# Attention slots of a gated cross-attention block: the product with the values placed ahead of the turns and projections on TensorE

## The chip, the core and the metric

The kernel runs on one core of a Trainium2 chip. The metric is device time in microseconds (us), the median of three runs. TensorE (PE in the profile) multiplies, VectorE (DVE), ScalarE (ACT) and GpSimd (POOL) work elementwise, and SyncE (SP) issues transfers. Each engine takes its own list of instructions in the order in which the program gives them, and they meet only at semaphores.

## The reference

`x` has 2 batches of 512 tokens of width 128; the context has 2 x 32 tokens of width 128. Queries come from the normalised `x`; keys and values come from the normalised context and from the normalised `x` itself. There are 16 heads of 64.

```
xn, ln = layernorm(ctx), layernorm(layernorm(x))
q = ln @ Wq
k, v = split(concat([xn @ Wkv, ln @ Wkv], axis=1))
sim  = rmsnorm(q) * scale @ rmsnorm(k).T
attn = softmax(sim)
x = x + tanh(g_xattn) * ((attn @ v) @ Wout + bout)
x = x + tanh(g_ffn) * moe(layernorm(x))      # 8 experts of width 256, top 2 of 8
```

The whole kernel works with each float32 operand split in a high and a low half of 16 bits, so one product in full precision is three matmuls (high by high, high by low, low by high).

## The kernel before, in words

**Units and slots.** A unit is 4 heads of one batch; there are 8 units of 8 slots, 64 attention slots in all (`SLOTS`). Slot n works on head `n % 8 // 2` of unit `n // 8` and on one half of its 512 keys. Each engine has a function `slot(n)`, and its list is the unrolled loop over n; the tables `qk_at`, `t_at`, `v_at`, `cs_at`, `nm_at` and `cst_at` say what else is done in which slot. So the order of the work is written out by hand.

**What TensorE does in slot n, before.** First the transposed scores of slot n: four matmuls (lines 1234, 1235) into `st_ps`, which wait until ScalarE has taken slot n-1's out of it (`exp_ok`). Then `score(j)`, two matmuls (line 1175) for the row maxima of a slot 11 later. Then, in even slots up to 44, `turn_tile`: four transposes (line 1163) of a projected and normalised tile of queries and keys, into `tv`; and in even slots up to 42 `project_tile`: three matmuls (lines 1093 to 1095) for the tile that is turned two slots later, into `pj`. In every other odd slot the three matmuls make values instead. Then `times_values(n - 2)`: 16 matmuls of the exponentials' high half (lines 1150, 1151), 8 of their low half (line 1156), and in odd slots 12 more for the context. The low half is waited for right before line 1156 (`plo_ok`). In slots 8u+4 and 8u+5 follow the context's scores and the turn of the maxima, in slots 8u the context's transposed scores.

**What follows a turn and a projection.** ScalarE in slot n takes the exponential of slot n (line 656), then the high halves of the turned tile (lines 603, 604), then the squares of the projected tile (line 589). VectorE in slot n divides a finished head (lines 963, 970), takes the maxima of `score` (line 941), the low halves of the turned tile (line 840), the sums of squares (line 819) and the mean squares (line 823). In slot n+1 GpSimd raises the mean squares to the power -1/2 (`inverse_rms`, line 439), and VectorE multiplies the projected tile by the result (`normalise_qk`, line 829), which slot n+2's turn waits for. In slots with new values VectorE takes their low half behind that (line 985).

**GpSimd's list** in slot n is: `inverse_rms` of slot n-1's projection, if there was one; then the low half of slot n-1's exponentials, `p_lo` (line 516); in slots 8u+2 also the low half of the context's exponentials, `pc_lo` (line 522). It takes the rms first and the low half second, in this order.

**After slot 44** there are no turns of queries and keys; the attention's output is turned and projected, and experts follow (lines 1358 to 1377 on TensorE, 560 on GpSimd).

Of the kernel before, what the change touches and what calls it, by code (L numbers as in the profile page):

```python
# [21 lines left out]
def flamingo_gated_block(nc, x, ctx_in, mask, g_xattn, g_ffn, ln_x_g, ln_x_b, ln_l_g, ln_l_b, qn_g, kn_g,  # L22
# [20 lines left out]
    with ExitStack() as ctx:  # L43
# [149 lines left out]
        def need(eng, s, count):  # L193
            if count > 0:
                eng.wait_ge(s, count)
# [38 lines left out]
        def need_lo(eng, k):  # L234
            on_dve, on_pool = lo_counts(k)
            need(eng, lo_ok, on_dve)
            need(eng, lop_ok, on_pool)

        def need_vlo(eng, k):
            need(eng, vlop_ok, min(k, QT))  # L240
            need(eng, vlo_ok, k - QT)

        def is_slot(n):
            return 0 <= n < SLOTS
# [13 lines left out]
        def o_part(G, q):  # L258
            return o_ps[G % 2][:, (DH + 1) * q:(DH + 1) * (q + 1)]
# [812 lines left out]
        def _(pe):  # L1072
# [13 lines left out]
            def project(out_ap, toks, w):  # L1086

                if isinstance(w, tuple):
                    hi, lo = (m[:, :].rearrange("p (g k c) -> p g k c", g=NG, k=3)[:, w[0]:w[0] + w[1], 2, :]
                              for m in (wqkv_hi, wqkv_lo))  # L1090
                else:
                    hi, lo = wqkv_hi[:, w], wqkv_lo[:, w]
                nc.tensor.matmul(out_ap, lnT_hi[:, toks], hi, start=True, stop=False)
                nc.tensor.matmul(out_ap, lnT_hi[:, toks], lo, start=False, stop=False)
                return nc.tensor.matmul(out_ap, lnT_lo[:, toks], hi, start=False, stop=True)
# [50 lines left out]
            def values(o_of, ph, cols, vh, vl, start):  # L1146

                for q in range(QT):
                    c = slice(cols.start + q * P, cols.start + (q + 1) * P)
                    nc.tensor.matmul(o_of(q), ph[:, c], vh, start=start and q == 0, stop=False, skip_group_check=True)  # L1150
                    nc.tensor.matmul(o_of(q)[:, 0:DH], ph[:, c], vl, start=False, stop=False, skip_group_check=True)  # L1151

            def values_lo(o_of, pl, cols, vh):
                for q in range(QT):
                    c = slice(cols.start + q * P, cols.start + (q + 1) * P)
                    last = nc.tensor.matmul(o_of(q), pl[:, c], vh, start=False, stop=True, skip_group_check=True)  # L1156
                return last

            def turn_tile(tau):
                pe.wait_ge(norm_ok, tau + 1)  # L1160
                tr = turn_bank(tau)
                for c in range(4):
                    last = nc.tensor.transpose(tr[:, c * P:(c + 1) * P], qk[tau % 2][:, c * P:(c + 1) * P], ident[:, :])  # L1163
                last.then_inc(qkT_ok, 1)

            def score(j):
                u, c, q = j // 8, j % 8 // QT, j % QT
                if j == 0:
                    pe.wait_ge(norm_ok, QT)
                if j % 8 == 0:  # L1170
                    pe.wait_ge(hi_ok, QT * (u + 1))
                need(pe, mx_ok, j)
                for r in range(2):
                    rows = slice(DH * r, DH * (r + 1))
                    last = nc.tensor.matmul(s2_ps[:, 512 * r:512 * (r + 1)], HL[u % 2][rows, 0, c, q * P:(q + 1) * P],  # L1175
                                            HL[u % 2][rows, 0, 2 + c, :], start=True, stop=True)
                last.then_inc(s_ok, 1)
# [9 lines left out]
            def times_values(m):  # L1187
                u, h, i = m // 8, m % 8 // 2, m % 2
                G = m // 2
                if i == 0:  # L1190

                    need(pe, o_ok, G - 1)
                    if h == 0:
                        pe.wait_ge(cexp_ok, u + 1)
                    if h == 2 and u + 1 < UNITS:
                        pe.wait_ge(nmc_ok, u + 2)
                need_vlo(pe, QT * (u // 2) + 2 * i + 2)
                pe.wait_ge(exp_ok, m + 1)

                def o_of(q):  # L1200
                    return o_part(G, q)

                for k in range(2):
                    v = V[u // 2 % 2][:, 2 * i + k, HG * (u % 2) + h, :]
                    values(o_of, p_hi[m % NP], slice(512 * k, 512 * (k + 1)), v[:, 0:DH + 1], v[:, DH + 1:VW],
                           i == 0 and k == 0)
                if i == 1:
                    v = Vbd[u % 2][:, h, :]
                    if h == 0:
                        pe.wait_ge(vbd_ok[u % 2], 64 * (u // 2 + 1))  # L1210
                        pe.wait_ge(cplo_ok, u + 1)
                    values(o_of, pc_hi[u % 2], slice(0, 512), v[:, 0:DH + 1], v[:, DH + 1:VW], False)
                    values_lo(o_of, pc_lo[u % 2], slice(0, 512), v[:, 0:DH + 1])
                pe.wait_ge(plo_ok, m + 1)
                for k in range(2):
                    v = V[u // 2 % 2][:, 2 * i + k, HG * (u % 2) + h, :]
                    last = values_lo(o_of, p_lo[m % NP], slice(512 * k, 512 * (k + 1)), v[:, 0:DH + 1])
                last.then_inc(pv_ok, 1)

            def slot(n):  # L1220
# [17 lines left out]
                j = s_pair(n)  # L1238
                if j is not None:
                    score(j)  # L1240
                if n in t_at:
                    tau = t_at[n]

                    need_lo(pe, tau)

                    need_vlo(pe, len([m for m in v_at if m < n]))
                    if n > LN1_AT + 4:
                        pe.wait_ge(lnT_ok, 3)
                    turn_tile(tau)
# [12 lines left out]
                if n in v_at:  # L1262
# [7 lines left out]
                        pe.wait_ge(wlo_ok, NG)  # L1270
                    g, first = 2 * w % NG, 2 * w // NG * N + t * P
                    project(tv[:, :], slice(first, first + P), (g, 2)).then_inc(v_mm, 1)
                if is_slot(n - 2):
                    times_values(n - 2)
                if n == CTX_AT:

                    pe.wait_ge(wlo_ok, NG)
# [103 lines left out]
            for n in range(FIRST, LAST):  # L1381
                slot(n)
                if n in (SLOTS, SLOTS + 1):
                    gate_up(n - SLOTS)
# [47 lines left out]
```

## Time and profile before

| | us |
|---|---|
| median of 3 runs | 387.31 (385.56 to 388.3) |
| the profiled execution | 387.43 |
| its span in the trace | 385.6 |
| TensorE busy | 320.4 |
| GpSimd busy | 256.5 |
| VectorE busy | 292.4 |
| turn of slot 4 to turn of slot 44 | 89.66 to 220.64 |

In the rows a time is in microseconds from the span's start. A row of the timeline gives the start, the duration, the engine, the line of the kernel, the operation, the tile written, the tiles read, their shapes and, in square brackets, how long the engine sat idle before it and what ended that. A matmul's duration is longer than the distance to the next, because they are pipelined, so distances between starts tell TensorE's pace. A matmul over 512 columns in the attention stage follows the one before by 0.22 us.

### The profile page before, as it was taken

To read this page: it belongs to the slowest core of one execution; us is meant where nothing else is said; L and a number is where in the kernel's file an instruction comes from. 1 tells how busy PE (TensorE), PEld (TensorE's weight loads), DVE (VectorE), ACT (ScalarE), POOL (GpSimd) and SP (SyncE) were. 2 spreads that over 40 slices of the span, in tenths; PEclk is the share of its full clock that TensorE was granted. 3 is DMA by queue.
4 is the path that set the end of the run, shared out by engine and by line. 5 is a ranking of instruction groups with operands and counts; after the bars stand their busy time and mean duration, and the time that the engine had idled before them with its cause. 6 is when DMAs were issued, how large, how long until landed. Compare 5 with 4: busy or idle time off the path is not lost.

```text
span 385.6 us, 9369 instructions
## 1 busy us (share of the span) xinstructions
PE 320.4 (83%) x3641; PEld 197.9 (51%) x3641; DVE 292.4 (76%) x578; ACT 195.3 (51%) x329; POOL 256.5 (67%) x197
## 2 busy tenths in 40 slices
PE   1563756789999999999999999899865999965993
PEld 0131423346556556555555656687543787533662
DVE  4874756769888898888898974646796677888895
ACT  2532434555665565656555645366824454624451
POOL 7695368478797897888887987356932334523453
PEclk9956686789999999999999999999996999999999
DMA  6316000620530611603406116730000000001000
GB/s 191 92 30 134 3 7 2 133 42 2 117 60 5 149 27 25 148 6 86 91 6 141 33 29 145 225 112 3 2 2 0 2 2 0 3 0 29 0 3 28
DMA packets 31470, 20.38 MB, mean 53 GB/s; under 512 B 11650, under 2 KB 30914, under 8 KB 31426
## 3 DMA queue, kind: packets, MB, share of 16 engines
q1 hardware_dynamic: 30482, 19.75, 22.4%
q8 instruction: 29, 0.48, 0.5%
q10 hardware_dynamic: 944, 0.04, 0.2%
q14 instruction: 15, 0.12, 0.1%
HBM read 5.87 MB, written 0.52 MB: 17 GB/s over the span
## 4 chain that ended last, share of the span: by engine, by line
POOL 31%; issue 28%; PE 22%; DVE 12%; ACT 4%; DMA 1%; POOLq 1%; DVEq 0%; ACTq 0%
POOL p_lo L516 18%; POOL p_lo L560 5%; POOL rms_r L439 3%; PE pj L1128 3%; DVE wqkv_hl L1033 2%; PE tv L1163 2%; POOL pc_lo L522 2%; PE tv L1113 1%; DVE sumsq L819 1%; PE big L1358 1%; PE big L1360 1%; POOL v L534 1%; PE big L1359 1%; PE big L1234 1%; DVE qk L829 1%
## 5 line engine op out<-in xcount | busy, mean ns | idle before, releaser
L516 POOL TENSOR_TENSOR p_lo<-p 128x1024 f16<-128x1024 f32 x64 | 121.9, 1924 | 17.2 <-ACT p L656 13.3
L656 ACT ACTIVATE p<-big 128x1024 f32<-128x1024 f32 x64 | 65.6, 1025 | 66.0 <-PE big L1235 63.9
L941 DVE TENSOR_REDUCE nm_main<-big 128x2 f32<-128x1024 f32 x64 | 78.2, 1222 | 20.2 <-PE big L1175 19.8
L560 POOL TENSOR_TENSOR p_lo<-p,p_lo 128x512 f16<-128x512 f32 x32 | 37.1, 1159 | 58.6 <-ACT p_lo L735 56.3
L439 POOL TENSOR_TENSOR rms_r<-meansq,power 128x8 f32<-128x8 f32 x32 | 52.3, 1638 | 29.1 <-DVE meansq L823 28.3
L1234 PE MATMUL big<-w 128*128 128x512 f16 x128 | 48.8, 381 | 2.7 <-ACT p L656 2.7
L1235 PE MATMUL big<-w 68*128 68x512 f16 x128 | 48.7, 380 | 0.0
L1150 PEld LDWEIGHTS o_ps<-v,p 128*128 128x128 bf16 x512 | 35.9, 99 | 9.4 <-issue 4.1
L1150 PE MATMUL o_ps<-v,p 128*128 128x65 f16 x512 | 40.7, 194 | 0.0
L1151 PE MATMUL o_ps<-v,p 128*128 128x64 f16 x512 | 40.6, 195 | 0.0
L1151 PEld LDWEIGHTS o_ps<-v,p 128*128 128x128 bf16 x512 | 34.4, 98 | 5.5 <-issue 0.3
L1175 PE MATMUL big<-hl 64*128 64x512 f16 x128 | 26.0, 402 | 9.2 <-DVE nm_main L941 9.2
L1046 DVE SCALAR_TENSOR_TENSOR p<-p,big 128x512 f32<-128x512 f32 x32 | 21.8, 683 | 15.0 <-ACT p L730 14.9
L1163 PE MATMUL tv<-ident,qk 128*128 128x128 f32 x116 | 20.8, 307 | 14.8 <-DVE qk L829 8.1
L1358 PE MATMUL big<-x2T_hi,gu_hi 128*128 128x512 f16 x64 | 25.2, 394 | 8.7 <-DVE p L1050 8.7
L1373 PE MATMUL o_ps<-wd_hi,p_lo 128*128 128x128 f16 x128 | 23.8, 223 | 8.6 <-POOL p_lo L560 5.6
L730 ACT ACTIVATE p<-big 128x512 f32<-128x512 f32 x32 | 18.9, 594 | 22.0 <-PE big L1360 20.7
L819 DVE TENSOR_REDUCE sumsq<-squares 128x8 f32<-128x512 f32 x32 | 21.7, 678 | 9.0 <-ACT squares L589 8.9
L1156 PE MATMUL o_ps<-v,p_lo 128*128 128x65 f16 x512 | 26.2, 194 | 0.3 <-POOL p_lo L516 0.3
L1163 PEld LDWEIGHTS tv<-ident,qk 128*128 128x128 f32 x116 | 13.5, 152 | 22.9 <-issue 20.0
L1359 PE MATMUL big<-x2T_lo,gu_hi 128*128 128x512 f16 x64 | 25.3, 395 | 0.0
L1360 PE MATMUL big<-x2T_hi,wqkv_hl 128*128 128x512 f16 x64 | 25.1, 391 | 0.0
(206 smaller groups left out, 758.7 us busy)
## 6 DMA issues: line engine op xcount, KB each, us to landing
w<-hl SPq DMA_DIRECT2D x64, 128.0 KB, 3.4
w<-hl SPq DMA_DIRECT2D x16, 256.0 KB, 3.9
hl<-n_kernel_gating_EDF_dram SPq DMA_DIRECT2D x1, 1024.0 KB, 5.8
hl<-L_ffn_kernel_up_EDF_dram SPq DMA_DIRECT2D x1, 1024.0 KB, 5.4
o_sb<-in_L_xattn_Wkv_dram SPq DMA_DIRECT2D x2, 384.0 KB, 7.2
x_sb<-in_x_dram SPq DMA_DIRECT2D x2, 256.0 KB, 4.0
wout<-in_L_xattn_Wout_dram SPq DMA_DIRECT2D x1, 512.0 KB, 4.8
k1c<-kc_hl SPq DMA_DIRECT2D x32, 8.0 KB, 1.8
```

The source lines that it names most:

```text
L439: nc.gpsimd.tensor_tensor(rms_r[:, tau % QT, :], meansq[:, tau % QT, :], power[:, 0:8], ALU.pow).then_inc(rr_ok, 1)
L516: nc.gpsimd.tensor_tensor(p_lo[m % NP][:, :], p[m % NP][:, :], p_hi[m % NP], ALU.subtract).then_inc(plo_ok, 1)
L560: nc.gpsimd.tensor_tensor(hid_lo[m % NH], hid[m % NH], hid_hi[m % NH], ALU.subtract).then_inc(hlo_ok, 1)
L656: nc.scalar.activation(p[n % NP][:, :], st_ps, ACT.Exp).then_inc(exp_ok, 1)
L941: nc.vector.tensor_reduce(nm_main[:, u % 2, 2 * c:2 * c + 2, q], s2_ps.rearrange("p (k n) -> p k n", k=2), AX_X, ALU.max, negate=True).the ...
L1150: nc.tensor.matmul(o_of(q), ph[:, c], vh, start=start and q == 0, stop=False, skip_group_check=True)
L1151: nc.tensor.matmul(o_of(q)[:, 0:DH], ph[:, c], vl, start=False, stop=False, skip_group_check=True)
L1163: last = nc.tensor.transpose(tr[:, c * P:(c + 1) * P], qk[tau % 2][:, c * P:(c + 1) * P], ident[:, :])
L1234: nc.tensor.matmul(o, w1[:, 2 + h // 2, h % 2, keys], w1[:, h // 2, h % 2, :], start=True, stop=False)
L1235: last = nc.tensor.matmul(o, w2[0:M_ROWS, 2 + h // 2, h % 2, keys], w2[0:M_ROWS, h // 2, h % 2, :], start=False, stop=True)
L1358: nc.tensor.matmul(o, gu_hi[k][:, w], x2T_hi[:, toks], start=True, stop=False)
L1359: nc.tensor.matmul(o, gu_hi[k][:, w], x2T_lo[:, toks], start=False, stop=False)
```

## The change

`times_values(n - 2)` stands right behind `score(j)`, ahead of the turn and of the projections. Nothing is added or removed, and the other engines' lists stay as they are. In slots without a turn or a projection the order is the same as before.

```diff
@@ -1238,6 +1238,8 @@
                 j = s_pair(n)
                 if j is not None:
                     score(j)
+                if is_slot(n - 2):
+                    times_values(n - 2)
                 if n in t_at:
                     tau = t_at[n]
 
@@ -1270,8 +1272,6 @@
                         pe.wait_ge(wlo_ok, NG)
                     g, first = 2 * w % NG, 2 * w // NG * N + t * P
                     project(tv[:, :], slice(first, first + P), (g, 2)).then_inc(v_mm, 1)
-                if is_slot(n - 2):
-                    times_values(n - 2)
                 if n == CTX_AT:
 
                     pe.wait_ge(wlo_ok, NG)
```

TensorE's list in slot 4 before, with the semaphores that each row waits for. Where lines are left out, the pair of lines 1150 and 1151 repeats seven times:

```order
L1175 MATMUL big<-hl 128x512
L1163 MATMUL tv<-ident,qk 128x128 [waits vlo_ok,lnT_ok,vlop_ok,norm_ok,lop_ok,lo_ok]
L1163 MATMUL tv<-ident,qk 128x128 x3
L1093 MATMUL pj<-wqkv_hl,lnT_hi 128x512 [waits norm_ok,wlo_ok]
L1094 MATMUL pj<-wqkv_hl,lnT_hi 128x512
L1095 MATMUL pj<-wqkv_hl,lnT_lo 128x512
L1150 MATMUL o_ps<-v,p 128x65 [waits exp_ok,vlop_ok]
L1151 MATMUL o_ps<-v,p 128x64
...
L1156 MATMUL o_ps<-v,p_lo 128x65 [waits plo_ok]
L1156 MATMUL o_ps<-v,p_lo 128x65 x7
L1304 MATMUL o_ps<-mask_row,ones_row 128x512 [waits o_ok,w1_ok1,kc_ok1]
```

The turn waited for the normalised tile (`norm_ok`) and for `tv` to be free (`vlo_ok`, `lo_ok`); the low half's wait (`plo_ok`) stood behind turn and projection. The same slot in the change:

```order
L1175 MATMUL big<-hl 128x512
L1150 MATMUL o_ps<-v,p 128x65 [waits exp_ok,vlop_ok]
L1151 MATMUL o_ps<-v,p 128x64
...
L1156 MATMUL o_ps<-v,p_lo 128x65 [waits plo_ok]
L1156 MATMUL o_ps<-v,p_lo 128x65 x7
L1163 MATMUL tv<-ident,qk 128x128 [waits vlo_ok,lnT_ok,vlop_ok,norm_ok,lop_ok,lo_ok]
L1163 MATMUL tv<-ident,qk 128x128 x3
L1093 MATMUL pj<-wqkv_hl,lnT_hi 128x512 [waits norm_ok,wlo_ok]
L1094 MATMUL pj<-wqkv_hl,lnT_hi 128x512
L1095 MATMUL pj<-wqkv_hl,lnT_lo 128x512
L1304 MATMUL o_ps<-mask_row,ones_row 128x512 [waits o_ok,w1_ok1,kc_ok1]
```

Now the turn and the projection stand behind the wait for `plo_ok`. GpSimd's list in slots 1 to 6, which the change leaves alone:

```order
L439 TENSOR_TENSOR rms_r<-meansq,power 128x8 [waits norm_ok,ms_ok]
L516 TENSOR_TENSOR p_lo<-p 128x1024 [waits exp_ok] x2
L522 TENSOR_TENSOR pc_lo<-pc 128x512 [waits cexp_ok]
L439 TENSOR_TENSOR rms_r<-meansq,power 128x8 [waits norm_ok,ms_ok]
L516 TENSOR_TENSOR p_lo<-p 128x1024 [waits exp_ok] x2
L439 TENSOR_TENSOR rms_r<-meansq,power 128x8 [waits norm_ok,ms_ok]
L516 TENSOR_TENSOR p_lo<-p 128x1024 [waits pv_ok,exp_ok] x2
```

In each pair of slots the rms of the even slot's projection (which waits for the mean squares, `ms_ok`) stands ahead of the low half of the even slot's exponentials.

## Rows read from the trace of the kernel before

**Rows 1.** The page, busy time of each engine over the whole span.
```profile
PE 320.4 (83%) x3641; PEld 197.9 (51%) x3641; DVE 292.4 (76%) x578; ACT 195.3 (51%) x329; POOL 256.5 (67%) x197
```

**Rows 2.** One unit: length; busy PE, PEld, DVE, ACT, POOL; clock, DMA share, GB/s.
```profile
163.80:190.00 26.20, 25.50 (x352) 15.23 (x351) 22.69 (x41) 15.31 (x24) 22.32 (x13) 1.00 0.32 66
```

**Rows 3.** Waits of 111.4 to 190 us (three units): total, times, longest.
```profile
POOL rms_r L439 <- DVE meansq L823: 11.1, 9, 1.5
...
PE tv L1163 <- DVE v L985: 1.3, 3, 0.5
...
PE tv L1163 <- issue: 0.6, 3, 0.2
```

**Rows 4.** Chain of waits of 163 to 193 us, its shares by line.
```profile
by line: POOL p_lo L516 52.2%; issue 47.5%; POOL pc_lo L522 6.6%; POOL rms_r L439 2.3%; POOLq L195 0.5%
```

**Rows 5.** Timeline of TensorE in slot 34, a slot without a wait.
```profile
187.43 0.39 PE L1175 MATMUL big<-hl 64*128 64x512 f16 x2
187.75 0.66 PE L1163 MATMUL tv<-ident,qk 128*128 128x128 f32 x4
...
188.68 0.38 PE L1095 MATMUL pj<-wqkv_hl,lnT_lo 128*128 128x512 f16 x1
...
189.39 0.40 PE L1156 MATMUL o_ps<-v,p_lo 128*128 128x65 f16 x8
...
189.63 0.38 PE L1234 MATMUL big<-w 128*128 128x512 f16 x1
```

**Rows 6.** Timeline of all engines from slot 36's score to slot 38's turn.
```profile
193.66 0.39 PE L1175 MATMUL big<-hl 64*128 64x512 f16 x2
...
194.47 0.63 PE L1163 MATMUL tv<-ident,qk 128*128 128x128 f32 x4 [0.42 <-DVE v L985]
...
195.78 0.60 ACT L589 ACTIVATE squares<-pj 128x512 f32<-128x512 f32 x1
...
197.35 0.17 DVE L823 TENSOR_SCALAR meansq<-sumsq 128x8 f32<-128x8 f32 x1
...
197.60 1.64 POOL L439 TENSOR_TENSOR rms_r<-meansq,power 128x8 f32<-128x8 f32 x1 [1.10 <-DVE meansq L823]
...
199.20 1.89 POOL L516 TENSOR_TENSOR p_lo<-p 128x1024 f16<-128x1024 f32 x1
...
201.27 0.66 PE L1163 MATMUL tv<-ident,qk 128*128 128x128 f32 x4
```

**Rows 7.** Timeline of GpSimd and VectorE in slot 35, ahead of slot 36's turn.
```profile
191.15 1.64 POOL L439 TENSOR_TENSOR rms_r<-meansq,power 128x8 f32<-128x8 f32 x1
...
192.82 0.69 DVE L829 TENSOR_TENSOR qk<-pj,rms_r 128x512 f32<-128x512 f32 x1 [0.56 <-POOL rms_r L439]
193.43 0.68 DVE L985 SCALAR_TENSOR_TENSOR v<-tv,v 128x512 f16<-128x512 f32 x1
```

**Rows 8.** Timeline of slots 1 to 3; last, the stretch's busy times and clock.
```profile
80.95 3.75 POOL L516 TENSOR_TENSOR p_lo<-p 128x1024 f16<-128x1024 f32 x2
...
81.86 1.00 PE L1163 MATMUL tv<-ident,qk 128*128 128x128 f32 x4 [0.51 <-DVE qk L829]
...
85.81 1.64 POOL L439 TENSOR_TENSOR rms_r<-meansq,power 128x8 f32<-128x8 f32 x1
...
82.00:84.00 2.00, 2.00 (x8) 1.11 (x8) 1.18 (x2) 0.83 (x3) 2.00 (x2) 0.50 0.11 21
```

**Rows 9.** Timeline of TensorE: slot 4's turn, slot 44's turn, slot 45's first matmul.
```profile
89.66 0.66 PE L1163 MATMUL tv<-ident,qk 128*128 128x128 f32 x4
...
220.64 0.63 PE L1163 MATMUL tv<-ident,qk 128*128 128x128 f32 x4 [0.40 <-DVE v L985]
...
222.67 0.38 PE L1234 MATMUL big<-w 128*128 128x512 f16 x1
```

**Rows 10.** Timeline among the experts: GpSimd's low half, then TensorE, which waited.
```profile
348.37 1.16 POOL L560 TENSOR_TENSOR p_lo<-p,p_lo 128x512 f16<-128x512 f32 x1 [5.92 <-ACT p_lo L735]
...
349.58 0.10 PEld L1373 LDWEIGHTS o_ps<-wd_hi,p_lo 128*128 128x128 f16 x1 [2.67 <-POOL p_lo L560]
```

## The prediction, made before the result was known

> **What bounds the kernel now.** I read the page first: TensorE is busy for 320.4 us of 385.6, more than any other engine [rows 1]. The change touches only slots 2 to 47, so the next view is the table of busy times by unit of 8 slots. In one unit of 26.20 us TensorE is busy for 25.50, GpSimd for 22.32 and VectorE for 22.69, at full granted clock (1.00, which is 2.4 GHz) [rows 2]. The reader is to see that TensorE sets the pace there and that GpSimd is close behind. The chain of waits for the same stretch nevertheless names GpSimd's low halves (52.2%) and "issue" [rows 4]: it follows GpSimd's own list back and does not go over to what GpSimd waited for. So I take from it only that GpSimd is nearly as tight. The table of waits says what it waited for: nine times in three units, 11.1 us in all, for VectorE's mean squares before the rms [rows 3]. TensorE's own waits ahead of a turn are small: 1.3 us in three times for VectorE's `v`, 0.6 us in three times put down to issue [rows 3], so (1.3 + 0.6) / 3 = 0.63 us a unit.
>
> The pace that I compare with: slot 4's turn starts at 89.66 and slot 44's at 220.64 [rows 9], 20 pairs of slots in 130.98 us, 6.55 us a pair.
>
> **What the change removes.** A turn that waits for VectorE would now have the values' matmuls ahead of it as cover. In slot 36 the score starts at 193.66 and the turn at 194.47 [rows 6]; in slot 34, without a wait, they are 0.32 apart [rows 5]. The values' high half and low half take, from the last projection matmul's start to the next slot, 189.63 - 188.68 - 0.22 = 0.73 us [rows 5], more than the 0.49 of delay. If nothing else came in, 0.63 us a unit would be saved, five times, and the 0.51 at slot 2 [rows 8]: 3.7 us.
>
> **What the change adds.** The low half's wait now stands ahead of the turn and the projection, in every even slot. That ties together two chains that were apart, because GpSimd takes the rms of slot n's projection ahead of slot n's low half. The new ring, from a turn to the turn two slots later, with the trace's distances:
> - Turn to rms: slot 36's turn starts at 194.47. The projection follows it, ScalarE's squares start at 195.78, the mean squares at 197.35 and the rms at 197.60, where GpSimd had sat idle for 1.10 us [rows 6]. That is 3.13 us. TensorE's part of it (turn, then projection) moves as one block, so the distance stays.
> - Rms to low half: the low half of slot 36 starts at 199.20, 1.60 us later, and takes 1.89 us [rows 6]. The exponential that it needs belongs to the slot before and is long there; the order of GpSimd's list keeps it back.
> - GpSimd to TensorE: at the only kind of place where TensorE clearly waits for GpSimd, the low half ends at 348.37 + 1.16 = 349.53 and the weight load starts at 349.58 [rows 10]. 0.05 us, and about 0.03 more to the matmul.
> - The low half's eight matmuls: 189.39 to 189.63, 0.24 us [rows 5]. Then comes slot 38's turn.
>
> The sum is 3.13 + 1.60 + 1.89 + 0.08 + 0.24 = 6.94 us. What the change of kind from the values' matmuls to the transposes costs is not shown; between score and turn the distance of 0.32 is 0.10 more than the 0.22 of 512 columns [rows 5], so it lies between 0 and 0.10. I take **6.95 us a pair**, near the lower end because the low half's hand-over may hide it.
>
> Is that ring the longest? TensorE's own work in the heaviest pair, slot 36's turn to slot 38's with the context's scores between, is 201.27 - 194.47 = 6.80 us without a wait inside [rows 6]; the mean pair has (26.20 - 0.63) / 4 = 6.39. Both are under 6.95. The old ring through VectorE's normalised tile is shorter too: from the rms at 191.15 to `v` at 193.43 and the turn at 194.47 is 3.32 [rows 6, 7], and 3.13 + 3.32 = 6.45. GpSimd's longest pair holds one rms (1.60), two low halves (2 x 1.85) and `pc_lo` (1.0): 6.3. So the new ring decides in all 20 pairs, and TensorE waits ahead of the low half: on average 6.95 - 6.39 = 0.56 us a pair. Today no ring runs through rms and low half together, since the low half is used behind the projection, and what waits behind it is not the next rms.
>
> **The terms.**
> 1. Slots 4 to 44: 20 x (6.95 - 6.55) = +8.0 us.
> 2. Start: slot 0's low half ends about 80.95 + 1.90 = 82.85 [rows 8]. Slot 2's turn was at 81.86 and can now start only behind it and the eight matmuls, which at the clock of 0.50 (1.2 GHz) in that place [rows 8] take up to twice 0.24. So the turn is 1.3 to 1.5 us later. Its rms was at 85.81, 3.95 behind the turn [rows 8], since turn and projection ran at the lower clock. If the clock is back earlier relative to the work, some of it returns. Between +0.5 and +1.5; I take +1.2, near the delay that must arise.
> 3. End: behind slot 44's turn the values (0.73) no longer stand before slot 45's first matmul, 222.67 - 220.64 = 2.03 us later today [rows 9]: -0.7 us.
> 4. Moved odd slots (the projection of values behind the product): nothing. Slot 35's `v` on VectorE stands behind the rms's `qk` anyway [rows 7], and its 3.32 us from rms to turn can grow to 3.82 before it reaches the new ring. If that cover went, each us counts once in every second pair.
>
> Sum: 8.0 + 1.2 - 0.7 = +8.5 us. The profiled execution took 387.43 us (span 385.6 and 1.8 around it), 0.1 above the median of 387.31, so the forecast is 395.9 on it and **395.8 us** on the median. Bounds: a pair of 6.80, where TensorE's heaviest pair alone decides, with a start of +0.5 gives +4.8 (392.1); a pair of 7.15, the ring with another 0.2 for each hand-over that the trace of before shows only among the experts, and a start of +1.5 give +12.8 (400.1).
>
> **The rivals.**
> - *The gain arrives* (9%): the low half is ready in time, the turns' waits vanish: 387.3 - 3.7 = 383.6 us, faster. It holds if, from a turn to the next low half, the ring is under 6.39 us. For it: the score of slot 36 at 193.66 plus 0.32 plus 0.5 of high half is 194.48, and the low half that it needs ends at about 191.15 + 1.60 + 1.90 = 194.65 [rows 6, 7], only 0.2 too late. Against it: the turn then starts later, and so do the rms and the next low half; the lateness is handed on until the pair is as long as the ring. The Trainium skill (Perfetto Trace Analysis, Identifying Performance Opportunities) says to improve the most occupied engine and to close the gaps in its row; by that, with TensorE at 25.50 of 26.20, this change would bring its 383.6. The trace speaks against it with GpSimd's share and its 11.1 us of waits.
> - *Delay is taken up* (6%): the ring lengthens by less than 0.15 a pair, or slots after 44 wait today for something that does not move. 387 to 391 us, within 1%. Against it: TensorE had no wait of length from slot 45's start on that would shrink, as far as the timeline of 222 to 236 us goes.
> - *The clock falls too* (4%): TensorE would now idle in every pair for 0.56 us of 6.95, 8%. At 0.50 slot 2's turn took 1.00 us where it takes 0.66 at full clock [rows 5, 8], and a pair's 6.39 us of work would near 10. Five of 20 pairs at that level are 5 x 3 = 15 us more: 411. Against it: clock 1.00 in the unit shown with 0.70 us of idleness in it. The Trainium skill (TensorE: Matmul & The Clock Gate, A second HAM failure mode) tells of a kernel whose clock swung because of many tiny pauses between groups of matmuls. By that rule this rival would be likely; no run here shows it yet.
> - *The ring decides*, as in the sum: 81%.
>
> **How the numbers follow.** The median is 395.8. The range 390 to 400.5 takes in both bounds and the lower edge of the second rival; outside lie the gain, most of the second rival and the clock, under 2 in 10. A measurement of this kernel tells 1% (3.9 us) from no change: its three runs lie within 0.7%. Slower by over 1% are the main case and the clock, 0.85; within 1% 0.06; faster 0.09.
>
> **What would show it.** In the new trace slots 4 to 44 should take about 139 us from turn to turn, evenly, also where no context work stands. TensorE should wait ahead of line 1156 for GpSimd's `p_lo`, in even slots only, and no more ahead of line 1163. GpSimd's wait before the rms for the mean squares should grow from 11.1 / 9 = 1.2 us to 6.95 - 1.60 - 2 x 1.87 = 1.6 us (less where `pc_lo` stands before it), its low half should start 1.60 behind the rms. The distance of turn to rms should stay 3.13. The forecast is wrong if the pairs keep 6.55, if the wait at line 1156 is absent, or if most of the difference lies after slot 45.

## The result and the profile after

| | before | after |
|---|---|---|
| median, us | 387.5 (385.56 to 388.3, 4 runs) | 396.11 (395.06 to 396.41, 4 runs) |
| the profiled execution, us | 387.43 | 395.98 |
| its span, us | 385.6 | 394.2 |
| ratio after / before | | 1.0225, 95% interval 1.0182 to 1.0267 |

The kernel before has one run more here than in the section on the time before, so its median is 387.5 and not 387.31. The forecast was 395.8, the measured median is 396.11, 2.25% slower and clear of noise. The three terms can be read off one by one. First TensorE's timeline of the change: slot 4's turn, slot 44's turn, slot 45's first matmul, which answer to [rows 9].

```profile
89.60 0.63 PE L1163 MATMUL tv<-ident,qk 128*128 128x128 f32 x4
...
229.93 0.63 PE L1163 MATMUL tv<-ident,qk 128*128 128x128 f32 x4
...
231.22 0.38 PE L1234 MATMUL big<-w 128*128 128x512 f16 x1
```

From slot 4 to slot 44 it now takes 140.33 us, 7.02 a pair, where it took 130.98 and 6.55. Slot 4's turn is as early as before, slot 45 starts 8.55 us later than before, and the span ends 8.6 later: behind slot 45 nothing was lost or regained.

One turn of the ring, slots 28 to 30, in the timeline of all engines. It answers to [rows 6].

```profile
173.77 0.63 PE L1163 MATMUL tv<-ident,qk 128*128 128x128 f32 x4
...
176.90 1.64 POOL L439 TENSOR_TENSOR rms_r<-meansq,power 128x8 f32<-128x8 f32 x1 [1.67 <-DVE meansq L823]
...
178.50 1.89 POOL L516 TENSOR_TENSOR p_lo<-p 128x1024 f16<-128x1024 f32 x1
...
180.45 0.42 PE L1156 MATMUL o_ps<-v,p_lo 128*128 128x65 f16 x8
...
180.79 0.63 PE L1163 MATMUL tv<-ident,qk 128*128 128x128 f32 x4
```

Turn to rms 3.13, rms to low half 1.60, low half to TensorE's first use of it 1.95 (1.89 and 0.06 of hand-over), that to the next turn 0.34: 7.02. ScalarE had finished the exponential that this low half needs at 173.03, 5.5 us before the low half started; GpSimd sat idle for 1.67 us ahead of the rms, with the low half behind it in its list. The table of waits, for three units of the change (117.7 to 201.8 us), shows both ends; it answers to [rows 3].

```profile
POOL rms_r L439 <- DVE meansq L823: 17.1, 12, 1.7
...
PE o_ps L1156 <- POOL p_lo L516: 5.0, 9, 0.6
```

TensorE waits for the low half 9 times in 12 pairs, 0.55 us each, and nowhere ahead of line 1163. In the other three pairs, those with the context's scores (as in the rows above), TensorE has more work of its own and arrives just as the low half does. The 12 waits of GpSimd for the mean squares are 1.67 us in nine pairs and 0.67 in the three in which `pc_lo` (1.0 us) stands ahead of the rms. The clock did not fall in this stage: here is the row of the busy times for the three units, as in [rows 2].

```profile
117.70:201.80 84.10, 78.47 (x1043) 46.12 (x1054) 66.67 (x121) 46.61 (x72) 67.05 (x40) 1.00 0.30 62
```

The granted clock is 1.00 (2.4 GHz) with TensorE busy for 93% of the stretch.

### The profile page after: what moved, and what is told of

It reads as the page before. It is cut to its first block, busy times and chain, and to the rows that moved or that the text cites. A ratio compares the mean times of both kernels' runs of the same rounds, so it can differ in the third digit from the quotient of the medians.

```text
span 394.2 us, 9345 instructions
## 1 busy us (share of the span) xinstructions
PE 320.8 (81%) x3617; PEld 197.8 (50%) x3641; DVE 288.6 (73%) x578; ACT 196.4 (50%) x329; POOL 256.4 (65%) x197
## 4 chain that ended last, share of the span: by engine, by line
POOL 35%; issue 26%; PE 21%; DVE 12%; ACT 4%; DMA 1%; POOLq 1%; DVEq 0%; ACTq 0%
POOL p_lo L516 23%; POOL p_lo L560 5%; PE pj L1128 2%; POOL rms_r L439 2%; DVE wqkv_hl L1033 2%; PE tv L1163 2%; POOL pc_lo L522 2%; PE tv L1113 1%; DVE sumsq L819 1%; PE big L1358 1%; PE big L1360 1%; PE big L1359 1%; POOL v L534 1%; PE big L1234 1%; PE big L1235 1%
## 5 line engine op out<-in xcount | busy, mean ns | idle before, releaser
L1150 PEld LDWEIGHTS o_ps<-v,p 128*128 128x128 bf16 x512 | 33.8, 99 | 13.0 <-issue 11.5
L603 ACT ACTIVATE hl<-tv,q_gain 128x256 f16<-128x256 f32 x29 | 13.7, 473 | 47.7 <-PE tv L1163 47.7
L1151 PEld LDWEIGHTS o_ps<-v,p 128*128 128x128 bf16 x512 | 34.1, 97 | 1.4
L840 DVE SCALAR_TENSOR_TENSOR hl<-tv,q_gain,hl 128x256 f16<-128x256 f32 x25 | 12.1, 484 | 23.9 <-ACT hl L604 23.9
L829 DVE TENSOR_TENSOR qk<-pj,rms_r 128x512 f32<-128x512 f32 x26 | 17.9, 689 | 13.4 <-POOL rms_r L439 13.4
```

## The experiments

Times are medians, ratios are against the kernel before on the same chip, with their 95% intervals. The kernel before has medians of 385.91 to 387.5 us on the chips used, so the ratios compare more closely than the times. A pair is the distance of two turns, two slots apart, and each profile has 20 of them from slot 4 to slot 44.

**Even slots alone, odd slots alone.** In the block that the change moved:

```diff
-                if is_slot(n - 2):
+                if is_slot(n - 2) and n % 2 == 0:      # even_only; n % 2 == 1: odd_only
                     times_values(n - 2)
...
+                if is_slot(n - 2) and n % 2 != 0:      # odd_only: n % 2 != 1
+                    times_values(n - 2)
                 if n == CTX_AT:
```

> The product with the values stands ahead of the turn and the projection in even slots only; in odd slots, behind the projection of values, as before. Theory: the ring runs through the even slots' low half alone, so the whole change is here: 395 to 397 us, 7.0 us a pair. Rival (the odd slots' later projection of values, and VectorE's low half of it behind, holds the next turn): under 392 us.

> The other part alone: ahead of the projection of values in odd slots, behind turn and projection in even slots. Theory: no cost, 386 to 388.5 us, 6.5 to 6.6 us a pair. Rival (odd slots carry the cost): 391 us or more.

Even slots alone: 397.12 us, ratio 1.0280 (1.0227 to 1.0332), just above the range of the theory; its 20 pairs took 140.53 us, 7.03 each, against 140.33 in the full change, so the whole effect is there, as the theory had it. Odd slots alone: 389.21 us, ratio 1.0093 (1.0052 to 1.0135). That is some 3 us slower and fits neither the theory nor the rival. Its 20 pairs took 133.59 us, 2.6 more than before, and only every second pair grew, the one in which values are projected: from 6.48 and 6.70 to about 6.83 and 6.90. The timeline of that kernel from slot 31's rms to slot 32's turn says why; it answers to [rows 7]:

```profile
179.02 1.64 POOL L439 TENSOR_TENSOR rms_r<-meansq,power 128x8 f32<-128x8 f32 x1 [1.48 <-DVE meansq L823]
...
181.00 0.61 ACT L683 ACTIVATE v<-tv 128x512 f16<-128x512 f32 x1 [1.16 <-PE tv L1095]
...
181.63 0.69 DVE L985 SCALAR_TENSOR_TENSOR v<-tv,v 128x512 f16<-128x512 f32 x1 [0.25 <-ACT v L683]
...
182.72 0.52 PE L1163 MATMUL tv<-ident,qk 128*128 128x128 f32 x3 [0.56 <-DVE v L985]
```

The values are projected later, ScalarE's high half of them ends at 181.61, VectorE waits 0.25 us for it, and the turn, which needs `tv` free, comes 3.70 us behind the rms where it was 3.32. In the full change this does not show, because there the turn comes 3.89 us behind the rms anyway (176.90 to 180.79).

**GpSimd's order, in the changed kernel and in the kernel before.**

```diff
-                if n - 1 in qk_at:
-                    inverse_rms(qk_at[n - 1])
                 m = n - 1
                 if is_slot(m):
...
                                             ALU.subtract).then_inc(plo_ok, 1)
+                if n - 1 in qk_at:
+                    inverse_rms(qk_at[n - 1])
```

> The changed kernel, and in GpSimd's list of each odd slot the low half of the exponentials now stands ahead of the rms. Theory (the new ring of turn, mean squares, rms, low half and turn costs the time): the low half no longer waits for the mean squares, the ring falls apart, TensorE's waits before line 1156 vanish, and the pairs go back to TensorE's own work or to the old ring, 6.4 to 6.55 us: 384 to 387.5 us. Rival (the order on TensorE costs the time by itself, by turning and projecting later, whatever GpSimd does): about 396 us stays, 7.0 us a pair.

> The kernel before, with the same exchange in GpSimd's list (low half ahead of the rms). Theory: without the low half in a ring with the turn the exchange frees nothing on TensorE; the pairs stay at 6.5 to 6.6 us, 386 to 389 us. Rival (GpSimd's order costs something in the kernel before too): 3 us or more below the kernel before. It also shows whether the clock of slot 2 falls in the old order of TensorE.

In the changed kernel the exchange brings the time back: 386.3 us, ratio to before 0.9981 (0.9959 to 1.0003), with TensorE's order untouched. In the kernel before it does nothing: 387.53 us, ratio 0.9999 (0.9973 to 1.0024), and the 20 pairs take 131.00 us as before. The clock in slot 2, which this run was also to show, was 1.00. So the cost belongs to the two orders together, TensorE's and GpSimd's. The timeline around slot 28's turn in the first of the two:

```profile
164.29 1.64 POOL L439 TENSOR_TENSOR rms_r<-meansq,power 128x8 f32<-128x8 f32 x1
...
166.88 0.41 PE L1156 MATMUL o_ps<-v,p_lo 128*128 128x65 f16 x8
...
167.62 0.63 PE L1163 MATMUL tv<-ident,qk 128*128 128x128 f32 x4 [0.32 <-DVE v L985]
```

The low half does not hold TensorE any more, yet the turn again waits for VectorE's `v`, 3.33 us behind the rms. The product with the values stands ahead of the turn and fills part of the wait (0.32 us are left where the kernel before had 0.4), but the turn starts no earlier behind the rms. This kernel is at the old pace, 26.18 us a unit.

**The high half first, the low half where it was.**

```diff
+            def times_values_lo(m):          # the second part of times_values, from the wait for plo_ok on
...
                 if is_slot(n - 2):
                     times_values(n - 2)      # high half and context only
                 if n in t_at:
...
+                if is_slot(n - 2):
+                    times_values_lo(n - 2)
                 if n == CTX_AT:
```

> The changed kernel, but only the high half's products stand ahead of the turn and the projection; the wait for the low half and its products stand behind them, as before. Theory: the ring through the low half is cut, while the 0.5 us of high half covers the turn's waits of 0.63 us a unit: 384 to 387 us, the wait before line 1163 gone, pairs of 6.39 to 6.5 us. Rival (any values' work ahead of the turn makes the turn, the squares and the rms late): 390 us or more.

386.73 us, ratio 0.9982 (0.9960 to 1.0005); one unit takes 26.17 us. The ring through the low half is cut and the cost is gone, as expected. The wait ahead of line 1163 is gone too, all but 0.22 us in one of 20 pairs, and still the pairs did not shrink to the 6.39 to 6.5 us expected: they take 6.55 on average. The turns that need `v` come 3.32 or 3.33 us behind the rms in nine of ten such pairs, as before. Covering the wait does not shorten the ring that it comes from.

**Turn, product, projection.** The block moves from ahead of the turn to behind it; in odd slots, which have no turn, it stays ahead of the projection of values:

```diff
                     turn_tile(tau)
+                if is_slot(n - 2):
+                    times_values(n - 2)
                 if n in qk_at:
```

> In even slots the turn first, then the product with the values with its wait, then the projection. Theory: the ring still runs through the low half, but from the projection on: without the turn's 0.47 us and the 0.10 of changing kind, 7.01 - 0.5 to 0.6 = 6.4 to 6.5 us, about TensorE's own work with its old waits before the turn (6.39 + 0.16 a pair): 386 to 389 us. Rival (every wait for the low half ahead of anything that feeds the rms costs the full amount): 394 us or more.

392.97 us, ratio 1.0161 (1.0125 to 1.0198): outside what the theory gave, and below what the rival gave. TensorE has no wait for the low half in slots 6 to 44 of this trace. The timeline of slots 30 to 32:

```profile
178.92 0.66 PE L1163 MATMUL tv<-ident,qk 128*128 128x128 f32 x4
...
182.60 1.64 POOL L439 TENSOR_TENSOR rms_r<-meansq,power 128x8 f32<-128x8 f32 x1 [1.48 <-DVE meansq L823]
...
184.88 0.68 DVE L985 SCALAR_TENSOR_TENSOR v<-tv,v 128x512 f16<-128x512 f32 x1
...
185.92 0.63 PE L1163 MATMUL tv<-ident,qk 128*128 128x128 f32 x4 [0.71 <-DVE v L985]
```

Turn to rms has grown from 3.13 to 3.68, by the product between turn and projection; rms to turn is 3.32 as before. That makes this pair 7.00 us: the old ring, through VectorE and not through the low half, has become the long one. It holds only in every second pair, those with new values (7.00, and 7.23 where `pc_lo` stands ahead of the rms and puts it off to 3.91); the pairs between take 6.80 and 6.19, as in the kernel before. The mean is 6.80 against 6.55. My expectation had shortened one ring and forgotten that the other contains the same stretch.

**A dose inside the ring.** A memset between rms and low half:

```diff
+        idle = sb("idle", [P, 22, 256], U8)
...
                     inverse_rms(qk_at[n - 1])
+                    if is_slot(n - 1):
+                        nc.gpsimd.memset(idle[:, (n - 1) // 2, :], 0)
```

> The changed kernel with a memset of 256 bytes a partition on GpSimd between the rms and the low half, of perhaps 0.2 to 0.3 us, in each of 22 odd slots. Theory: it lies inside the ring, so every one counts in full: 396.1 + 21 x 0.2 to 0.3 = 400 to 402.5 us, a pair of 7.01 plus the memset's time in the trace. Rival (GpSimd has slack in every pair, and the cost lies on TensorE's order alone): 395 to 397.5 us.

> The kernel before with the same 22 memsets. Theory: no ring runs through rms and low half together, so a memset counts only where the next rms comes right behind pc_lo, once a unit: 5 x 0.3 = 1.5 us at most, 386 to 389 us. Rival (GpSimd sets the pace in the kernel before too): 391 to 394 us.

GpSimd in the changed kernel with the dose, one round:

```profile
159.76 1.64 POOL L440 TENSOR_TENSOR rms_r<-meansq,power 128x8 f32<-128x8 f32 x1 [1.67 <-DVE meansq L826]
161.34 0.31 POOL L514 MEMSET idle<- 128x256 uint8 x1
161.61 3.74 POOL L519 TENSOR_TENSOR p_lo<-p 128x1024 f16<-128x1024 f32 x2
```

The low half starts 1.85 us behind the rms, 0.25 later than without. Slots 4 to 44 took 91.19 to 236.64 us, 7.27 a pair, 0.25 more: the dose counts in full, although GpSimd still sits idle for 1.67 us ahead of the rms in three of four pairs. The median is 403.13 us, 1.0412 (1.0373 to 1.0450), 7 us over the changed kernel and just above the expected range. In the profiled execution 5.6 us of the 7.7 us of difference in the span are the dose's (5.1 in the 20 pairs, 0.5 between slot 2's score and slot 4's turn). Of the rest 1.1 us lie ahead of slot 2's score and 1.0 behind slot 45, outside the stretch in which the theory has the doses count; their cause is not shown.

In the kernel before the same dose gives 389.35 us, 1.0061 (1.0035 to 1.0087), some 2.4 us, also just above the expected range. Its 20 pairs took 132.33 us, 1.35 more than before, and that is in the one pair of each unit in which `pc_lo` stands ahead of the rms (6.95 to 7.12, before 6.69 to 6.76), as the theory had it with its at most 1.5 us. The other 1 us is not accounted for.

**The old ring.** On VectorE, in odd slots with new values:

```diff
-                if n - 1 in qk_at:
+                late = n in v_at and v_at[n] >= QT
+                if n - 1 in qk_at and not late:
                     normalise_qk(qk_at[n - 1])
...
                                                    op1=ALU.subtract).then_inc(vlo_ok, 1)
+                if n - 1 in qk_at and late:
+                    normalise_qk(qk_at[n - 1])
```

> The kernel before; on VectorE, in odd slots with new values, the low half of the values now stands ahead of the multiplication by the rms, in the time in which VectorE waited for the rms. Theory (in the kernel before the turn's waits are the ring turn, mean squares, rms, qk, v, turn, and not missing cover): the ring loses up to 0.6 us in every second pair, TensorE's 0.63 us of waits a unit go: 384 to 386 us. Rival (the waits come from elsewhere): 386.5 to 388 us.

> A version that could beat both: the product with the values ahead of the turn in even slots only, low half ahead of the rms on GpSimd, low half of the values ahead of qk on VectorE. Theory: neither ring binds, TensorE works through at 25.5 to 25.6 us a unit: 383.5 to 386 us, no slower than vlow_before. Rival (the later turn in even slots costs something even without both rings): 388 us or more.

The kernel before with this edit alone: 382.26 us, ratio 0.9874 (0.9845 to 0.9902), faster than forecast and the fastest here. With the product with the values ahead of the turn in even slots and GpSimd's low half ahead of the rms added, it is the same, 382.34 us, 0.9876 (0.9845 to 0.9907). Its timeline around slot 28's turn, which answers to [rows 7], and the busy times of one of its units:

```profile
161.50 1.64 POOL L439 TENSOR_TENSOR rms_r<-meansq,power 128x8 f32<-128x8 f32 x1
...
162.77 0.69 DVE L986 SCALAR_TENSOR_TENSOR v<-tv,v 128x512 f16<-128x512 f32 x1 [0.16 <-ACT v L683]
...
163.38 0.68 DVE L829 TENSOR_TENSOR qk<-pj,rms_r 128x512 f32<-128x512 f32 x1
...
164.33 0.66 PE L1166 MATMUL tv<-ident,qk 128*128 128x128 f32 x4
...
151.90:177.37 25.47, 25.47 (x354) 15.23 (x352) 22.75 (x41) 15.08 (x25) 22.39 (x14) 1.00 0.33 68
```

`v` now runs while the rms is still being made, the turn comes 2.83 us behind the rms where it was 3.32, and it waits for nothing. TensorE is busy for all 25.47 us of the unit, against 25.50 of 26.20 before. The forecast had counted 0.63 us a unit; it is 0.73 (20 pairs in 127.34 us, where they took 130.98), and slots 2 to 4, which it had left out, gained as well: from slot 2's turn to slot 4's 6.45 us, against 7.26 in two kernels with VectorE's old order and a clock of 1.00 there (GpSimd's exchange in the kernel before, odd slots alone).

**The same edit in the changed kernel,** with the changed kernel once more beside it:

> The changed kernel itself once more, as the reference for the next one on the same chip: 395 to 397 us, 7.01 us a pair.

> The changed kernel with the low half of the values ahead of qk on VectorE, the edit that took 4 us or so off the kernel before. Theory: the pairs are set by the ring through GpSimd's low half, in which neither v nor qk stands, and qk has 3.8 us of room behind the rms; nothing changes: 395 to 397 us, 7.01 us a pair. Rival (the two gains and costs simply add, since both concern the turn's waits): 391 to 393 us.

396.3 us for the changed kernel, 1.0248 (1.0187 to 1.0309); 396.35 with the edit, 1.0255 (1.0199 to 1.0311); pairs of 7.02 in both. The edit that is worth over 4 us where the old ring sets the pace is worth nothing where the ring through the low half does.

## Why the prediction was right, and where it was not

- **What bounds the stage, and the new ring.** Right. Each link has its number in the rows after, and three kinds of edit show it: cutting the ring on GpSimd or on TensorE takes the whole cost away, a dose inside it counts in full, and a gain on the other ring counts nothing.
- **Term 1, +8.0.** Measured +9.35. The mis-sized link is the change of kind from the values' matmuls to the transposes: it was set at 0.01 within bounds of 0 to 0.10 and is 0.10 (0.34 from line 1156 to line 1163, where 0.24 was taken). The other links were off by 0.03 at most. 7.02 lay at the end of the bound, not near the lower one.
- **Term 2, +1.2.** Measured -0.06 between the two profiles, yet the delay arose as forecast. From slot 2's score to its turn it took 0.89 us before (80.97 to 81.86) and 2.19 after (80.36 to 82.55), 1.30 more, where 1.3 to 1.5 was forecast. Two differences hid it that the change did not make. Slot 2's score, ahead of which nothing was moved, came 0.61 us earlier; in a second profile of the changed kernel it stands at 81.22, so this place differs by as much from one execution to another. And in the profile of before the clock stood at 0.50 in slot 2 [rows 8], in that of the change at 1.00. From slot 2's score to slot 4's turn the change takes 9.24 us and the kernel before, at the lower clock, 8.69. Three kernels in which TensorE takes the low half behind the turn in slot 2, as before, and whose clock was 1.00 there, take 8.16, 8.17 and 8.16 (GpSimd's exchange in the kernel before, odd slots alone, high half first). So at one clock the new order costs about 1.1 us at the start, inside the bounds of 0.5 to 1.5, and the low clock had cost the profile of before about 0.5. The reason given for the 3.95 us from slot 2's turn to its rms was wrong: at full clock it is 3.94 and 3.95 in the second and third of these kernels, because GpSimd takes `pc_lo` first. In the change, where the turn itself is later, it is 3.13.
- **Term 3, -0.7.** Measured 1.29 - 2.03 = -0.74.
- **The sum.** -0.06 + 9.35 - 0.74 is 8.55, as forecast (8.5); terms 1 and 2 missed in opposite directions by 1.3 each, so the hit is closer than the working. Part of that is luck: had both profiles had the same clock and the same start, the sum would have come to about 1.1 + 9.35 - 0.74 = 9.7 (an estimate from the rows above), still inside the range. The rival in which the delay is taken up behind slot 44 fell with this: slot 45 starts 8.55 us later and the span ends 8.6 later.
- **Term 4, the odd slots.** In the full change they cost nothing; even slots alone cost as much. Their room is real but thin: without the new ring they cost 3 us.
- **The old ring, 6.45.** Right for one pair, too short for another. I added slot 36's 3.13 from turn to rms to slot 35's 3.32 from rms to turn. In the pair that ends with slot 36's turn, though, `pc_lo` stands ahead of the rms, and from slot 34's turn at 187.75 [rows 5] to the rms at 191.15 [rows 7] there are 3.40 us: that ring is 6.72. Nothing in the sum hung on it, since both lie under the new ring.
- **What the change removes** was misread. I counted 0.63 us a unit that cover could save. The turn's waits came from the old ring, which is longer than TensorE's own work in those pairs, and cover does not shorten a ring. With the new ring cut, the product ahead of the turn brought 0.2% (0.9981 and 0.9982, both intervals reach 1.00, so it is not clear of noise), while the shorter old ring brought 1.3%.
- **The rivals.** "The gain arrives" fell for a second reason besides the one given: with the low half in time (GpSimd's exchange in the changed kernel) it did not come either. For the clock the row shows 1.00 at 93% busy in this stage. By the Trainium skill (TensorE: Matmul & The Clock Gate, A second HAM failure mode) the many pauses could have made it swing; this trace does not agree, with pauses of 0.55 us in three of four pairs.

## What to carry to other kernels

Before moving work ahead on one engine, write down every ring that its waits close, link by link over all engines, and compare each with the engine's own work per round: the longest sets the pace, and an engine with 1.67 us of idle time a round, as GpSimd here, can stand in the middle of it. A wait on the busiest engine is worth covering only if it is not itself part of such a ring; otherwise the ring has to be shortened, and what did it here was to look on each engine for an operation that waits behind one that is not ready, while its own inputs are. The old ring was shortened by exchanging two operations in VectorE's list, and nothing on TensorE.

## What the runs showed that was not expected

- Once a ring sets the pace the pairs repeat almost exactly: 7.01 or 7.02 us in nearly every pair of the change, whether it holds the work of a pair that took 6.2 or one that took 6.8 us before. Where TensorE's own work sets the pace the pairs differ by what they hold (6.21 to 6.82 us in the fastest kernel).
- From the low half's last matmuls to the first transpose there are 0.34 us in nearly every pair of the change, whether TensorE had waited or not; to a matmul over 512 columns there are 0.24 [rows 5].
- At the attention's start the clock of one and the same place was 0.50 in the profile of before and 1.00 in that of the change; the kernel with turn, product and projection in this order had 0.52 there, and all others 1.00. TensorE's order in slot 2 does not decide it alone: four other kernels with the order of before in that slot had 1.00. Each has one profile, and what decides it was not found.
